# Three of the eight decoder tiles made inside the cross attention instead of in the first write and the multiply stage

## What is computed

```
w_l = dequant_kbit(qweight, lut4, 4)         # idx = sum of 4 bit planes; w = lut4[row, idx]; 1024 x 1024
# cross block, after a layer norm of x
qkv_in = rat_read(h, attn_read_w, ..., 3)
attn   = attention(qkv_in, qkv_w, pos)       # q, k, v projections, rope, causal softmax, 16 heads
h      = rat_write(h, attn, ...)             # "first write"
mlp_in = rat_read(h, mlp_read_w, ..., 2)
mlp    = silu(g_in @ ctx[0].T) * (u_in @ ctx[1].T)
h      = rat_write(h, mlp, ...)              # "second write"
y      = layernorm(x + h) @ w_l.T + bias
```

## Time and profile before

| | |
|---|---|
| median of 3 runs | 1933.74 us (1928.92 to 1940.87) |
| profiled execution | 1936.91 us, span 1935.2 us |
| mean granted PE clock | 0.918 |
| busy | PE 84%, DVE 71%, ACT 47%, POOL 30% |

### The profile page before, as it was taken

One profiled execution on the slowest core, in us unless ns is written; L12 is line 12 of the kernel. 1 busy time (PEld: TensorE's weight loads), 2 busy tenths in 40 slices (PEclk: granted clock), 3 DMA queues, 4 the chain that ended last, 5 costly groups with the idle time before them and its releaser, 6 DMA issues. The chain is left out here.

```text
span 1935.2 us, 23526 instructions
## 1 busy us (share of the span) xinstructions
PE 1617.2 (84%) x6880; PEld 1062.2 (55%) x6880; DVE 1364.9 (71%) x2077; ACT 903.6 (47%) x1671; POOL 576.7 (30%) x460
## 2 busy tenths in 40 slices
PE   3679999999999899999999887558897567785599
PEld 2456666666666666666666654455564453343244
DVE  7558788777877777788788766664465775777851
ACT  2245445454454454544454442243467655667210
POOL 1045446345355355454455452103111000000000
PEclk9889999999999999999999999679899567887699
DMA  3111101101011111110101000406342000000111
GB/s 117 52 44 33 55 22 55 34 25 54 34 44 34 34 45 34 45 44 23 55 23 44 22 23 12 171 33 120 76 67 84 1 1 1 0 33 22 40 53 38
DMA packets 30982, 84.39 MB, mean 44 GB/s; under 512 B 6006, under 2 KB 7304, under 8 KB 30600
## 3 DMA queue, kind: packets, MB, share of 16 engines
q1 hardware_dynamic: 30856, 82.87, 14.6%
HBM read 70.27 MB, written 12.58 MB: 43 GB/s over the span
## 5 line engine op out<-in xcount | busy, mean ns | idle before, releaser
L492 DVE SCALAR_TENSOR_TENSOR acc<-pj,sc_o,acc 128x1024 f32<-128x1024 f32 x232 | 293.9, 1279 | 99.2 <-PE pj L623 92.4
L492 DVE SCALAR_TENSOR_TENSOR q_acc<-pj,sc_q,q_acc 128x1024 f32<-128x1024 f32 x224 | 286.7, 1280 | 40.3 <-PE pj L623 32.2
L602 POOL TENSOR_TENSOR prob<-prob,inv_total 128x512 f32<-128x512 f32 (+3 forms) x256 | 190.0, 746 | 400.1 <-DVE inv_total L537 400.1
L623 PE MATMUL pj<-ctx_hi,w_o 128*128 128x512 f32 x528 | 238.1, 451 | 28.7 <-DVE kv_acc L492 13.5
L623 PE MATMUL pj<-zT_hi,w_q 128*128 128x512 f32 x512 | 225.5, 441 | 2.4 <-DVE q_acc L492 2.0
L435 ACT ACTIVATE prob<-ps,low_max 128x512 f32<-128x512 f32 (+3 forms) x256 | 134.3, 527 | 163.4 <-DVE low_max L530 149.4
L676 PE MATMUL ps<-kT,qT 128*128 128x512 f32 (+3 forms) x512 | 187.2, 448 | 25.5 <-issue 14.0
L623 PE MATMUL pj<-ctx_lo,w_o 128*128 128x512 f32 x528 | 207.9, 394 | 0.0
L623 PE MATMUL pj<-zT_lo,w_q 128*128 128x512 f32 x512 | 203.6, 398 | 0.0
L700 PE MATMUL pv<-probT,v 128*128 128x512 f32 (+3 forms) x512 | 169.6, 433 | 0.0
L623 PEld LDWEIGHTS pj<-ctx_hi,w_o 128*128 128x128 f32 x528 | 99.1, 188 | 116.7 <-DVE acc L492 47.3
(11 more groups left out here) (309 smaller groups left out, 3116.5 us busy)
## 6 DMA issues: line engine op xcount, KB each, us to landing
raw_o<-in_w_o SPq DMA_DIRECT2D x33, 512.0 KB, 3.6
raw_q<-in_w_q SPq DMA_DIRECT2D x32, 512.0 KB, 3.6
x_ring<-qk_kept SPq DMA_DIRECT2D x64, 128.0 KB, 5.1
ln_x<-in_x SPq DMA_DIRECT2D x8, 512.0 KB, 6.5
raw_kv<-in_w_k SPq DMA_DIRECT2D x8, 512.0 KB, 3.5
raw_kv<-in_w_v SPq DMA_DIRECT2D x8, 512.0 KB, 3.9
x<-in_x SPq DMA_DIRECT2D x8, 512.0 KB, 6.4
x_kept<-x SPq DMA_DIRECT2D x8, 512.0 KB, 2.6
```

The lines of the kernel that those rows point to most:

```text
L492: dve.scalar_tensor_tensor(out=dst, in0=pj[slot][:], scalar=scale, in1=dst, op0=ALU.mult, op1=ALU.add).then_inc(evac_v, 1)
L602: pool.tensor_tensor(prob[:, k % PROBS, 0:w], prob[:, k % PROBS, 0:w], inv_total[:, n:n + 1].to_broadcast([P, w]), ALU.mult).then_inc(norm ...
L623: ins = pe.matmul(pj[slot][:, b * S:(b + 1) * S], lhs, part[:, b * S:(b + 1) * S], start=n == 0, stop=n == 1)
```

## The change

Tiles 0, 1 and 2 are made in the cross attention. Tile 0 (quarters 0 to 7) lies in its prologue: blends 0 to 2 follow ACT's `high` of rounds 0 to 2, blends 3 to 7 follow the first five `copy_v`; merges 0 to 2 lie between DVE's rounds, merges 3 to 7 behind the last one. Its scratch is pT, the tile that the exponentials write later. Tiles 1 and 2 (quarters 8 to 23) lie in the steps t = 28, 33, ... 103, one blend each at step t and its merge on DVE at step t + 1; scratch and sums are in the projection inputs (inT, a part of acc) and cos_r, which nothing reads any more by then. The first write makes one tile (3) instead of two: one quarter a step. There PE turns tiles 0, 1, 2 in steps 0, 1 and 2, right behind that step's products, and ACT copies them ahead of its blends; before, both turned tiles came behind the eight steps. The multiply stage makes two tiles (4, 5) instead of four: one quarter a step, one turn before step 9 and one at the end. The second write is as before. Sums and scratch are now held in a table per tile and per stage instead of two fixed buffers.

```diff
@@ constants
+X2_FROM = max(LATER) + 3
-W1_TILES, W2_TILES = (0, 1), (6, 7)
-Q_W1, Q_MLP, Q_W2, Q_END = 0, 16, 48, 64
+X_TILES, W2_TILES = (0, 1, 2), (6, 7)
+Q_X2, Q_W1, Q_MLP, Q_W2, Q_END = 8, 24, 32, 48, 64
+X2_AT = {X2_FROM + 5 * n: Q_X2 + n for n in range(Q_W1 - Q_X2)}
+HELD_BY = {4: 0, 5: 3, 6: 4, 7: 5}
@@ cross attention
+        deq.borrow(0, [pT[:, n] for n in range(N_S)])
+        free = cos_r[:].rearrange("p t r -> p (t r)")
+        deq.borrow(Q_X2, [inT[:, n // 2, HALF * (n % 2):HALF * (n % 2 + 1)] for n in range(8)]
+                   + [free[:, n * HALF:(n + 1) * HALF] for n in range(2)])
+        deq.sums[1], deq.sums[2] = inT[:, 4], inT[:, 5]
@@ DVE
                 low(r - 1)
+                deq.merge(dve, r - 1)
             low(3)
+            for q in range(3, Q_X2):
+                deq.merge(dve, q)
...
+                if t == X2_FROM:
+                    dve.wait_ge(proj, 2 * len(ROUNDS))
+                    dve.wait_ge(v_proj, NT)
+                if t - 1 in X2_AT:
+                    deq.merge(dve, X2_AT[t - 1])
@@ ACT
                 if r in (1, 2):
                     rows(r)
+                if r < 3:
+                    deq.blend(act, r)
...
                 copy_v(i)
+                if 3 + i < Q_X2:
+                    deq.blend(act, 3 + i)
+            act.wait_ge(deq.merged, 7 * Q_X2 // QUARTERS)
...
+                if t in X2_AT:
+                    deq.blend(act, X2_AT[t])
@@ multiply stage
-        turn_at = {5: 2, 9: 3, 13: 4}
+        turn_at = {9: 4}
@@ first write, PE
                     wr.delta(pe, i - 2)
-            for o in W1_TILES:
-                deq.turn(pe, o, p_w)
+                if i in X_TILES:
+                    deq.turn(pe, i, p_w)
+            deq.turn(pe, 3, p_w)
@@ first write, ACT
                     wr.copy_delta(act, i - 3)
+                if i in X_TILES:
+                    deq.copy(act, i, p_w, fT)
                 for q in range(w1_quarter(i), w1_quarter(i + 1)):
                     deq.blend(act, q)
             wr.soft(act, 0)
-            for o in W1_TILES:
-                deq.copy(act, o, p_w, fT)
+            deq.copy(act, 3, p_w, fT)
```

More of the change, by code:

```diff
@@ L1703, in __init__, with borrow, use, stage @@
         self.w = [sb(f"d_w{i}", [P, D])[:] for i in range(2)]
-        self.low = self.mask = self.part = self.pair = None
+        self.sums = {o: self.w[n] for n, held in enumerate(((0, 4, 6), (3, 5, 7))) for o in held}
+        self.low, self.mask, self.part, self.pair = {}, {}, {}, {}
         self.made, self.bits, self.low_done, self.mask_done, self.blended, self.merged, self.turned, self.copied = (
             sem(f"d_{n}") for n in ("made", "bits", "low", "mask", "blended", "merged", "turned", "copied"))
[L1708 to L1714, removed]
+    def borrow(self, first, tiles):
+        n = STAGES.index(first)
+        self.low[n] = [t.bitcast(I32) for t in tiles[0:2]]
+        self.mask[n] = [t.bitcast(I32) for t in tiles[2:5]]
+        self.part[n], self.pair[n] = tiles[5:8], tiles[8:10]
+    def use(self, first, name, ctx, nc):
         sb, _, _ = scope(nc, ctx)
-        self.borrow([sb(f"{name}t{i}", [P, HALF])[:] for i in range(10)])
+        self.borrow(first, [sb(f"{name}t{i}", [P, HALF])[:] for i in range(10)])
+    def stage(self, h):
+        return max(n for n, q in enumerate(STAGES) if q <= QUARTERS * h)
     def loads(self):
@@ L1740, in sum_of @@
     def sum_of(self, h):
-        return self.w[h // 2 % 2][:, HALF * (h % 2):HALF * (h % 2 + 1)]
+        return self.sums[h // 2][:, HALF * (h % 2):HALF * (h % 2 + 1)]
     def low_bit(self, dve, h):
-        t = self.low[h % 2]
+        t = self.low[self.stage(h)][h % 2]
         if h >= 2:
@@ L1780, in blend @@
                 act.wait_ge(self.merged, 7 * h + pair - 1)
-            dst = self.pair[pair % 2] if t else (self.part[pair - 1] if pair else self.sum_of(h))
-            act.activation(dst, self.low[h % 2], ACT.Identity, bias=self.lut[:, o, 2 * k:2 * k + 1],
+            n = self.stage(h)
+            dst = self.pair[n][pair % 2] if t else (self.part[n][pair - 1] if pair else self.sum_of(h))
+            act.activation(dst, self.low[n][h % 2], ACT.Identity, bias=self.lut[:, o, 2 * k:2 * k + 1],
                            scale=self.step[:, o, k:k + 1]).then_inc(self.blended, 1)
@@ L1791, in merge @@
         h, pair = q // QUARTERS, q % QUARTERS
-        total, part = self.sum_of(h), self.part
+        n = self.stage(h)
+        total, part, mask, other = self.sum_of(h), self.part[n], self.mask[n], self.pair[n]
         if pair == 0:
@@ L1797, in merge @@
         dve.wait_ge(self.blended, 8 * h + 2 * pair + 2)
-        self.keep(dve, part[pair - 1] if pair else total, self.mask[0], self.pair[pair % 2])
+        self.keep(dve, part[pair - 1] if pair else total, mask[0], other[pair % 2])
         if pair == 1:
             dve.wait_ge(self.merged, 7 * h + 2)
-            self.keep(dve, total, self.mask[1], part[0])
+            self.keep(dve, total, mask[1], part[0])
         if pair == 2 and QUARTERS * (h + 1) not in STAGES:
@@ L1805, in merge @@
             dve.wait_ge(self.merged, 7 * h + 5)
-            self.keep(dve, part[1], self.mask[1], part[2])
+            self.keep(dve, part[1], mask[1], part[2])
             dve.wait_ge(self.merged, 7 * h + 6)
-            self.keep(dve, total, self.mask[2], part[1])
+            self.keep(dve, total, mask[2], part[1])
     def turn(self, pe, o, pt):
```

22 lines of the change are left out of this document (11 added, 11 removed).

## The result

The changed kernel takes 1947.94 us (median of 11 runs, 1941.24 to 1951.22) where the kernel before takes 1933.74 (11 runs beside them). The ratio is 1.0071, interval 1.0056 to 1.0087: slower by 0.7%.

What follows compares the result with a forecast made beforehand. DVE was taken to bound the multiply stage, PE the cross attention's steps. Terms -28.4 + 9.4 + 10 + 3 + 12 + 3 = +9.0 on the profiled 1936.9 gave 1945.9, so a 1943 us median; range 1924 to 1966.

Steps and rivals of the forecast that it cites:

- Part 1: Multiply stage: DVE's decoder work halves, PE becomes the bound at 3.43 us a step; -28.4 us, bounds -31 and -25.
- Part 2: Cross attention's prologue: blends and merges delay copies of v and the first reduction; +9.4 us, bounds +5 and +14.
- Part 3: Cross attention's steps: twelve quarters delay reductions and exponentials, 1.0 us each, less 2 us absorbed; +10 us, bounds 3 and 18.
- part 6: Clock in prologue and steps: waits of 1.6 us may bring two falls, one net; +3 us, bounds 0 and 6.
- the ring's wait of 4.97 us: Cross attention, t = 33: PE waits for the ring's DMA anyway, so quarter 8's delay of some 3 us is free.
- Part 4: Cross attention's tail: blend pairs between exponentials that PE waits for; +3 us, bounds 1 and 5.
- Part 5: First write: products, transposes and copies wait on each other in steps 0 to 2; +12 us, bounds 7 and 19.
- half-clock case: First write: at half clock transposes and products take nearly twice as long; +15 us or more.
- What follows is not shortened: Behind the first write: two tiles' copies behind `soft` already lie beside DVE's `soft_sum` and reciprocal, so no gain.
- Rival of bursts that hide: Steps and first write: free time on DVE and ACT and two banks absorb bursts; sum -8, 1925 us; chance 0.20.
- Rival of the clock that falls again and again: Cross attention's steps: repeated waits drop PE to half clock, eight falls, +21 more, 1964 us; chance 0.25.
- Table loads: Cross attention's steps: Identity blends beside Exp bring two 1.28 us loads a quarter, some 41 us, about 1980; chance 0.01.

Runs made afterwards that it cites:

- The short run: Changed kernel with blends, masks, low bit and copies of the first three tiles (24 quarters) working on 32 of 512 columns: 1925.22 us, one execution.
- the run with short blends: Changed kernel with only ACT's blends in the cross attention's 16 steady-state quarters working on 32 of 512 columns, merges whole: 1947.42 us, one execution.
- the last experiment: Changed kernel with a quarter every fourth unit in place of every fifth, merges and blend pairs whole: 1946.16 us, ratio to before 1.0058.

## Why the prediction was right, point by point

The time (1943 forecast, 1947.9 measured) and the sign were right, and each stage that was given a change moved the way it was said to. The forecast of +9.0 on the profiled execution met +10.2. That the sum came so close is in part luck. The multiply stage gained 3.3 us more than forecast, and the first write lost 3.3 more. In the cross attention's steps my sum had the waits some 4 us too large and the clock some 9 too small.

- **Part 1, multiply stage: -28.4 predicted, -31.7 measured**, past my bound of -31. The walk was right (steps of 3.43 us, PE the bound, a turn before step 9 that cost 3.2 us, 8.3 us at the end); mis-sized were the fall of the clock that I added (1.5, it did not come) and the start, where the half level ended earlier (first Silu 5.2 us after the first products, 6.6 before). The wait for merges came to 5.3 us, just over the 5 that I had named.
- **Part 2, prologue: +9.4 and +10.5.** The copies of v behind blends were in the walk. The 3.1 us wait for a `rope` behind quarter 0's merge was not named there. The first reduction came 38.9 us after the block's start, where I had said 37. The short run gives the stage back (24.7 us).
- **Part 3 and 6, steps and clock: +13 together, +17.7 measured**, and split another way than I said. PE's idle time in the steps grew by 5.9 us: 8.2 more from group 3 on, 2.3 less in groups 0 to 2. Part 3 had 10. PE's busy time for nearly the same matmuls grew by 11.8 us, 9.7 of it in groups 0 to 2, where the granted clock fell from 0.92 to 0.76; part 6 had 3 and an upper bound of 6. From group 3 on, twelve quarters cost 8.2 us of waiting, 0.7 us a quarter and not 1.0. Against the run with short work (62.8 us there at a granted clock of 1.00, where the changed kernel has 75.6 at 0.95) the bursts cost 12.8: 7.6 of PE's waits and 5.2 of half level. So the bursts bring waits and also time at the half level, and I had priced one fall net for all the steps. That 12.8 is close to my 12 is luck. How much of the clock's part in groups 0 to 2 the change brings is open (last section). Quarter 8 did bring a wait, 2.7 us of PE for `copy_out`, but the ring's wait of 4.97 us was gone (in the short run 2.0 of it was left). So in idle time it was free, as said; what took the place of the ring's wait was PE's time at the half level.
- **Part 4, tail: +3 and +2.8.**
- **Part 5, first write: +12 and +15.3.** The mechanism was right, shown by its removal; the size is that of my half-clock case ("+15 or more"). PE's idle time grew by 3.6 us (10.8 in place of 7.2) and its busy time by 11.7 (42.6 in place of 30.9). Six groups of transposes that this stage did not have before, at 0.6 us each at full clock, make some 3.6 of that, so some 8 is the half level (an estimate from these rows).
- "What follows is not shortened" was 2.1 us off: one tile's copies fewer behind the softplus brought the first exponent 3.6 us nearer to it.
- **Rival of bursts that hide:** void, PE waited for them. **Rival of the clock that falls again and again:** void from group 3 on. In three groups with 5.5 us of PE idle time the granted clock was 0.96, and 1.00 in the run with short blends that still had 43.4 us. But what the clock cost in groups 0 to 2 (9.7 us) is of the size of two to three of the falls that this rival counted, at 4 us each. **Table loads:** no blend brought one; the cross attention has one load, as before. (The sum of that rival is 1984, not "about 1980".)
- The Trainium skill's rule ("TensorE: Matmul & The Clock Gate", "HAM oscillation"), that TensorE falls back only after long idle stretches, would have made parts 5 and 6 together 8 us. Part 5 alone came to 15.3, but there the rule isn't put to the test: both kernels start the block at the half level (first products of 2.71 us), and what differs is when full clock came back, with the products of step 1 before (1.43 us at 1479.24) and with those of step 6 after (1.43 us at 1548.04). In the steps the trace does not agree: the rows below show half level right behind a wait of 1.60 us.

In one respect I was too quick. The single 1.60 us wait of the earlier trace rows was my evidence that such a wait brings a fall. The changed kernel has that wait too, with the half level behind it. The same wait in the last experiment, whose program is the changed kernel's up to there, was followed by full clock. Timeline and windows, changed kernel first:

```profile
1369.04 0.80 PE L1285 MATMUL x_pe<-x_ring 128*128 128x512 f32 x1 [1.60 <-ACT x_pT L1453]
...
1369.00:1379.00 10.00, 9.96 (x43) 6.39 (x43) 3.47 (x8) 2.86 (x5) 0.00 (x0) 0.50 0.14 52
```

```profile
1367.82 0.50 PE L1285 MATMUL x_pe<-x_ring 128*128 128x512 f32 x1 [1.60 <-ACT x_pT L1453]
...
1364.00:1374.00 10.00, 8.21 (x57) 5.36 (x57) 6.43 (x14) 4.99 (x9) 1.26 (x1) 1.00 0.20 79
```

The wait alone does not decide. What does is open; no run here was made for it.

## What to carry to other kernels

Work moved to an engine that is idle in sum costs by the length of its bursts, not by its sum: cut to single operations between the operations that others wait for, the same work fell from 2.6 us a group to 0.1 in three groups of the steady state. A clock fall in the group ahead of them took 3 us back, so read the granted clock of every stage beside its waits. When a step both feeds and waits for a second engine, give a moved two-stage hand-over (transposes, copy, transposes, copy) one stage a step and let the copy lag a step; whole in one step it cost more than the decoder work taken away. And place moved work so that it ends before the stage's tail: with pieces at every fourth unit the tail was 5.2 us shorter.

## What the hardware showed that was not expected

- Eight of the profiled kernels have the same program up to t = 28. Seven of them ran group 1 of the cross attention in 25.2 to 25.3 us, the last experiment in 18.7, with 83 matmuls in either. First the changed kernel, at a granted clock of 0.70, then the last experiment, at 1.00:

```profile
1352.30:1377.70 25.40, 23.49 (x83) 12.73 (x82) 11.94 (x22) 8.37 (x11) 2.54 (x2) 0.70 0.11 41
```

```profile
1353.80:1372.50 18.70, 16.48 (x83) 9.06 (x82) 11.84 (x22) 8.38 (x11) 2.53 (x2) 1.00 0.16 58
```

  One profiled execution can thus be 7 us off in a stage that nothing touched. That is as much as several terms of the sum, and half of the 13 us by which the runs of that experiment are spread. The kernel before has one profiled execution only, so its 54.9 us for groups 0 to 2 may be off in the same way: how much of the change's +7.3 there would last is open.
- In the changed kernel's first write PE was busy 42.6 of 53.4 us and the clock stayed at the half level for most of it (0.58); with one group of transposes a step it was busy 27.5 of 30.7 us at 0.89. A stage at half clock looks busy: its 42.6 us and these 27.5 hold almost the same work (115 and 114 matmul records).
